# A graph network on one core: the first graph's adjacency by row block into four free banks, and matmuls of ones in PE's waits

## The reference

```python
def cheb(h, A, W, bias):              # layer 1: Chebyshev, 4 orders
    d = A.sum(-1) ** -0.5
    L = I - d[:, None] * A * d[None, :]
    P = [I, L, 2*L@L - I, 2*L@(2*L@L - I) - L]
    return sum((P[k] @ h) @ W[k] for k in range(4)) + bias

def att_layer(h, A, wv, bv, wk, bk, wq, bq):
    v, q, k = tanh(h @ wv + bv), tanh(h @ wq + bq), tanh(h @ wk + bk)
    return softmax((q @ k.T) * A - 9e15 * (1 - A)) @ v

# layer 2: h1 = tanh(h @ enc_w + enc_b); h2 = att_layer(h1); h3 = att_layer(h2);
#          a three-step MLP on [h2, h3]
# layer 3: d2 = (A.sum(-1) + 1) ** -0.5; relu((d2 * (A + I) * d2) @ h @ W)
# layer 4: t = A @ h; 1 where t > 0.5, else 0
```

## Time and profile before

| | |
|---|---|
| median of three runs | 871.86 us |
| the profiled execution | 873.75 us, its span 871.8 us |
| PE, DVE, ACT, POOL busy | 88%, 64%, 51%, 41% of the span |
| first round (graph 0 alone) | 0 to 55.8 us |
| second round | 55.8 to 104.9 us |
| a round in the middle | 49.0 us |

### The profile page before, as it was taken

How to read it: one execution, slowest core, us unless ns; L and a number is a source line. 1 busy time by engine, 2 the same in 40 slices (tenths; PEclk the granted TensorE clock), 3 DMA queues, 4 the chain that set the end, 5 groups by cost and what they waited for, 6 DMA issues and landing times.

```text
span 871.8 us, 11510 instructions
## 1 busy us (share of the span) xinstructions
PE 771.5 (88%) x3808; PEld 543.3 (62%) x3808; DVE 561.3 (64%) x1631; ACT 445.4 (51%) x929; POOL 357.0 (41%) x475
## 2 busy tenths in 40 slices
PE   3649799998999999998999999998999999998864
PEld 2426566675766766675766666675766666675533
DVE  3255667767676767767676767767676767765432
ACT  2035463737474563737474563737474563735430
POOL 3133434536162544536162544536162544532200
PEclk9869899999999999999999999999999999999995
DMA  6100100102010010201020010101020110000000
GB/s 166 45 0 1 43 14 1 61 1 61 1 61 2 21 41 0 61 1 61 1 62 1 18 44 1 61 1 62 1 61 1 18 44 1 7 1 6 1 7 6
DMA packets 29275, 22.77 MB, mean 26 GB/s; under 512 B 19488, under 2 KB 21024, under 8 KB 29216
## 3 DMA queue, kind: packets, MB, share of 16 engines
q1 hardware_dynamic: 29216, 22.03, 8.5%
HBM read 19.93 MB, written 2.10 MB: 25 GB/s over the span
## 4 chain that ended last, share of the span: by engine, by line
PE 52%; issue 16%; POOL 15%; DVE 12%; ACT 4%; POOLq 0%; DVEq 0%
PE turn_ps L1056 13%; PE pre_ps L936 8%; PE post_ps L936 4%; POOL rstd_pre L414 4%; PE pre_ps L953 4%; PE turn_ps L1039 3%; POOL k_lo L486 2%; PE pre_ps L899 2%; DVE h_nat_pre L709 2%; POOL centred_pre L417 2%; DVE score_ps L795 2%; PE qkv_ps L990 2%; DVE h_nat_pre L701 2%; PE qkv_ps L995 2%; PE post_ps L1071 2%
## 5 line engine op out<-in xcount | busy, mean ns | idle before, releaser
L589 ACT ACTIVATE negz<-negz,negmax 128x512 f32<-128x512 f32 x128 | 92.2, 720 | 63.9 <-DVE negmax L803 63.8
L414 POOL TENSOR_TENSOR rstd_post<-vareps_post,nhalf 128x4 f32<-128x4 f32 x32 | 32.8, 1024 | 209.6 <-DVE vareps_post L691 209.6
L1056 PE MATMUL turn_ps<-pt,v_n 128*128 128x512 f32 x256 | 115.2, 592 | 0.0
L795 DVE TENSOR_TENSOR score_ps<-score_ps,a_nat 128x512 f32<-128x512 f32 x128 | 89.1, 696 | 19.4 <-PE score_ps L1025 18.5
L936 PE MATMUL pre_ps<-at_hi,u_pair_pre 128*128 128x512 f32 x192 | 88.4, 461 | 7.2 <-DVE u_pair_pre L731 5.2
L548 ACT ACTIVATE y_t_pre<-pre_ps 128x512 f32<-128x512 f32 x48 | 28.7, 597 | 124.6 <-PE pre_ps L936 124.6
L803 DVE CUSTOM_DVE_ANT_0 negz<-score_ps,gate 128x512 f32<-128x512 f32 x128 | 88.6, 692 | 4.4
L414 POOL TENSOR_TENSOR rstd_pre<-vareps_pre,nhalf 128x4 f32<-128x4 f32 x32 | 33.9, 1060 | 130.7 <-DVE vareps_pre L691 130.7
L596 ACT ACTIVATE pt<-turn_ps 128x512 f32<-128x512 f32 x128 | 74.0, 592 | 17.7 <-PE turn_ps L1039 15.6
L1039 PEld LDWEIGHTS turn_ps<-ident,negz 128*128 128x128 f32 x512 | 61.1, 141 | 32.6 <-issue 16.1
L936 PE MATMUL pre_ps<-at_lo,u_pair_pre 128*128 128x512 f32 x192 | 79.3, 413 | 0.0
(11 more groups left out here) (138 smaller groups left out, 1791.5 us busy)
## 6 DMA issues: line engine op xcount, KB each, us to landing
a_nat<-in_adj SPq DMA_DIRECT2D x16, 1024.0 KB, 5.8
x_in<-in_x SPq DMA_DIRECT2D x16, 128.0 KB, 2.6
out<-x_out SPq DMA_DIRECT2D x16, 128.0 KB, 1.9
cheb_ws<-in_L_gnn_weight SPq DMA_DIRECT2D x2, 64.0 KB, 4.9
att_w<-in_L_gnn_a_wv SPq DMA_DIRECT2D x2, 64.0 KB, 2.5
att_w<-in_L_gnn_a_wk SPq DMA_DIRECT2D x2, 64.0 KB, 2.3
att_w<-in_L_gnn_a_wq SPq DMA_DIRECT2D x2, 64.0 KB, 2.2
bv_f<-in_L_gnn_a_bv SPq DMA_DIRECT2D x2, 64.0 KB, 2.7
```

Source lines behind the costliest of these rows:

```text
L414: gp.tensor_tensor(rstd[t][:], vareps[t][:], nhalf[:, 0:RB], ALU.pow)\
L589: sc.activation(probs[:, i, :], negz[:, i, :], ACT.Exp, bias=negmax[:, i:i + 1], scale=-1.0, accum_out=total[:, i:i + 1]).then_inc(probs_d ...
L795: ve.tensor_tensor(score_ps[i % 2][:], score_ps[i % 2][:], a_nat[s][:, i, :], ALU.mult)\
L1056: mm = te.matmul(turn_ps[0][:], v_n[a][:, j * P:(j + 1) * P], pt[:, j, :], start=(j == 0), stop=(j == RB - 1))
```

## The change

Five edits, of which four touch the first graph only.

1. A second table, `FIRST`, gives the order of the first round. In it ACT adds up rows first and copies the turned blocks last; DVE takes the weights' product between the splits.
2. The adjacency of graph 0 comes in four loads of one row block each, with a semaphore each. PE turns a row block as it lands, into four banks (`post_ps`, `qkv_ps`, `turn_ps`), so that a bank is complete only after the fourth row block. The transpose of h goes to `score_ps[0]`.
3. The six early weight loads are issued by ACT's queue instead of SP's. DVE's first statistics come ahead of them; the Chebyshev weights are combined behind the normalisation, the encoder's are split and the bias rows of layer 1 made behind the first fold (`cheb_fold3`), those of layer 2 behind the second.
4. `keep_busy` puts 72 matmuls of a 128x128 tile of ones with a 128x512 row of ones into PE's order of the first round, from 2 to 17 ahead of each step. They write `score_ps[1]`, which nothing reads then. POOL sets the row of ones in one more memset.
5. In every round POOL's `inverse_roots` becomes two steps: `roots` makes only the four columns that u needs, `more_roots` the rest, behind `cheb_u3`. DVE's `cheb_weights` waits for the first, `cheb_fold3` for the second.

The diff, cut to its core:

```diff
-        norm_cheb-0 add_cheb_bias-0 split_qk.1-1 mask_bias-1 inverse_roots-0 cheb_u3-0
+        norm_cheb-0 add_cheb_bias-0 split_qk.1-1 mask_bias-1 roots-0 cheb_u3-0 more_roots-0
         norm_gcn-2 split_qk.2-1 cheb_f0-0 norm_last-2 norm_enc-0
+        add_mlp_bias-0""".split(),
+}
+
+
+FIRST = {
+    "tensor": """
+        turn_a0-0 turn_a1-0 turn_a2-0 cheb_ht-0 turn_a3-0 cheb_weights-0 cheb_prop3-0 cheb_fold3-0
+        cheb_prop2-0 cheb_fold2-0 cheb_prop1-0 cheb_fold1-0 enc_ht-0 encode-0""".split(),
+    "scalar": """
+        row_sum0-0 row_sum1-0 row_sum2-0 cheb_ht-0 row_sum3-0 copy_at0-0 copy_at1-0 copy_at2-0
+        copy_at3-0 cheb_copy3-0 cheb_copy2-0 cheb_copy1-0 enc_ht-0 encode-0""".split(),
+    "vector": """
+        stats_cheb-0 norm_cheb-0 cheb_ht-0 split_at0-0 split_at1-0 cheb_weights-0 split_at2-0
+        split_at3-0 cheb_fold3-0 cheb_fold2-0 cheb_fold1-0 stats_enc-0 norm_enc-0
+        enc_ht-0""".split(),
+    "gpsimd": """
+        norm_cheb-0 add_cheb_bias-0 roots-0 cheb_u3-0 more_roots-0 cheb_f0-0 norm_enc-0
         add_mlp_bias-0""".split(),
 }
...
+        def wait_rows(eng, g, i):
+
+            if first(g):
+                eng.wait_ge(a_rows_in[i], 16)
+            else:
+                eng.wait_ge(a_loaded[g.slot], 16 * (g.round + (g.slot > 0)))
+
+        def at_bank(g, j):
+
+            return (post_ps, qkv_ps, *turn_ps)[j][:] if first(g) else pre_ps[:, j % 2, :]
+
+        def ht_bank(g, k):
+
+            return score_ps[0][:] if first(g) and k == 0 else pre_ps[:, 0, :]
...
+            order, fill = ([(entry[:-2], int(entry[-1])) for entry in table[engine]]
+                           for table in (ORDER, FIRST))
-                for name, age in order:
+                for name, age in fill if graphs[1:] == (None, None) else order:
...
-            load(Graph(0, 0), False)
+            sp.dma_start(x_in[0][:], x_d[0]).then_inc(x_loaded[0], 16)
+            for i in range(RB):
+                sp.dma_start(a_nat[0][:, i, :], adj_d[0][:, i, :]).then_inc(a_rows_in[i], 16)
             for s in range(SLOTS):
                 sp.sem_inc(x_out_free[s])
-            for to, what in early:
-                sp.dma_start(to, what).then_inc(early_in, 16)
...
+            gp.memset(ones_row[:], 1.0).then_inc(consts_done, 1)
...
-            def inverse_roots(g):
+            def roots(g):
 
                 pool.wait_ge(rowsums, 4 * g.n + 4)
+                gp.tensor_tensor(dinv[g.slot][:, 0:RB], rs[:, 0:RB], nhalf[:, 0:RB], ALU.pow)\
+                    .then_inc(root_done, 1)
+
+            def more_roots(g):
...
-                pool_pre.add(gp.tensor_tensor(d[:], rs[:], nhalf[:], ALU.pow))
+                pool_pre.add(gp.tensor_tensor(d[:, RB:], rs[:, RB:], nhalf[:, RB:], ALU.pow))
...
-                pool.wait_ge(dinv_done, g.n + 1)
+                pool.wait_ge(root_done, g.n + 1)
...
+            early = [(cheb_bs[:], cheb_b.rearrange("a b c -> (a b c)").partition_broadcast(P))]
+            early += [(half, enc_w) for half in (enc_ws[0:C], enc_ws[C:P])]
+            early += [(enc_bs[:], enc_b.rearrange("(h o) -> h o", o=1))]
+            assert len(early) == n_early
+            for half in (cheb_ws[0:C], cheb_ws[C:P]):
+                act.dma_start(half, cheb_w.rearrange("k o c d -> (o c) k d")).then_inc(cheb_in, 16)
+            for to, what in early:
+                act.dma_start(to, what).then_inc(early_in, 16)
...
+                    if i == 0 or first(g):
+                        wait_rows(act, g, i)
                     if i == 0:
-                        act.wait_ge(a_loaded[g.slot], 16 * (g.round + 1))
...
+            def split_weights(whole, high, low, made):
+
                 ve.tensor_copy(high[:], whole).then_inc(weights_split, 1)
-            dve.wait_ge(weights_split, 5)
-            for whole, high, low in splits:
+                dve.wait_ge(weights_split, made + 1)
                 ve.tensor_tensor(low[:], whole, high[:].bitcast(F32), ALU.subtract)\
                     .then_inc(weights_split, 1)
+
+            def combine_cheb_weights():
+
+                dve.wait_ge(cheb_in, 16 * n_cheb)
+                ve.scalar_tensor_tensor(cheb_ws[:, 2, :], cheb_ws[:, 3, :], 2.0, cheb_ws[:, 2, :],
+                                        ALU.mult, ALU.add).then_inc(weights_split, 1)
+                ve.tensor_tensor(cheb_ws[:, 1, :], cheb_ws[:, 1, :], cheb_ws[:, 3, :], ALU.subtract)\
+                    .then_inc(weights_split, 1)
...
             def cheb_norm(g):
                 norm_apply("pre", dve_pre, g, 0)
+                if first(g):
+                    combine_cheb_weights()
...
                 dve.wait_ge(cheb_ready, g.n + 1)
-                dve.wait_ge(dinv_done, g.n + 1)
+                dve.wait_ge(root_done, g.n + 1)
...
+                dve.wait_ge(dinv_done, g.n + 1)
...
+                if first(g):
+                    dve.wait_ge(early_in, 16 * n_early)
+                    split_weights(enc_ws[:], enc_hi, enc_lo, 5)
+                    set_bias_rows(0)
...
+                if first(g):
+                    set_bias_rows(1)
...
-            pe.wait_ge(consts_done, 7)
+            pe.wait_ge(consts_done, 8)
+
+            IDLE = {"turn_a0": 8, "turn_a1": 3, "turn_a2": 3, "cheb_ht": 2, "turn_a3": 2,
+                    "cheb_weights": 4, "cheb_prop3": 11, "cheb_fold3": 2, "cheb_prop2": 6,
+                    "cheb_fold2": 2, "cheb_prop1": 6, "cheb_fold1": 2, "enc_ht": 17, "encode": 4}
+
+            def keep_busy(g, step):
+
+                if first(g):
+                    for _ in range(IDLE[step]):
+                        te.matmul(score_ps[1][:], ones_bf[:], ones_row[:], start=True, stop=True)
+
+            def turn_first_rows(g, i):
+
+                keep_busy(g, f"turn_a{i}")
+                wait_rows(pe, g, i)
+                for j in range(RB):
+                    mm = te.transpose(at_bank(g, j)[:, i * P:(i + 1) * P],
+                                      a_nat[g.slot][:, i, j * P:(j + 1) * P], ident[:])
+                    if i == RB - 1:
+                        mm.then_inc(at_ready, 1)
 
             def turn_a(j):
                 def f(g):
-                    pe.wait_ge(a_loaded[g.slot], 16 * (g.round + 1))
-                    if j == 0 and follows(g):
-
-                        pe.wait_ge(h1_done, g.n)
+                    if first(g):
+                        turn_first_rows(g, j)
+                        return
                     if j >= 2:
                         pe.wait_ge(at_split, 4 * g.n + j - 1)
+                    wait_rows(pe, g, 0)
+                    if j == 0:
+
+                        pe.wait_ge(h1_done, g.n)
                     for i in range(RB):
-                        mm = te.transpose(pre_ps[:, j % 2, i * P:(i + 1) * P],
+                        mm = te.transpose(at_bank(g, j)[:, i * P:(i + 1) * P],
                                           a_nat[g.slot][:, i, j * P:(j + 1) * P], ident[:])
                     mm.then_inc(at_ready, 1)
                 return f
 
-            def turn_h(ready):
-
-                pe.wait_ge(h_ready["pre"], ready)
+            def turn_h(g, k):
+
+                pe.wait_ge(h_ready["pre"], 2 * g.n + k + 1)
                 for i in range(RB):
-                    mm = te.transpose(pre_ps[:, 0, i * P:(i + 1) * P],
+                    mm = te.transpose(ht_bank(g, k)[:, i * P:(i + 1) * P],
                                       h_nat["pre"][:, i, :, :].rearrange("p a c -> p (a c)"), ident[:])
                 mm.then_inc(ht_ready, 1)
 
             def cheb_ht(g):
-                pe.wait_ge(at_split, 4 * g.n + 3)
-                turn_h(2 * g.n + 1)
+                keep_busy(g, "cheb_ht")
+                if follows(g):
+                    pe.wait_ge(at_split, 4 * g.n + 3)
+                turn_h(g, 0)
 
             def cheb_weights(g):
+                keep_busy(g, "cheb_weights")
                 pe.wait_ge(ht_split, 2 * g.n + 1)
-                pe.wait_ge(at_split, 4 * g.n + 4)
                 if first(g):
-                    pe.wait_ge(weights_split, 7)
+                    pe.wait_ge(weights_split, 5)
+                else:
+                    pe.wait_ge(at_split, 4 * g.n + 4)
                 for i in range(RB):
                     w = (K - 1) * C
                     for part in (cheb_hi, cheb_lo):
@@ -955,21 +1040,35 @@
                 return mm
 
             def cheb_prop3(g):
+                keep_busy(g, "cheb_prop3")
+                if first(g):
+                    pe.wait_ge(at_split, RB)
                 pe.wait_ge(cheb_taken, 3 * g.n + 3)
                 propagate("pre", g, 3 * g.n + 1, pre_ps[:, 0, :])
 
             def cheb_prop(k):
-                return lambda g: propagate("pre", g, 3 * g.n + k, pre_ps[:, 0, :])
+                def f(g):
+                    keep_busy(g, f"cheb_prop{K - k}")
+                    propagate("pre", g, 3 * g.n + k, pre_ps[:, 0, :])
+                return f
 
             def cheb_fold(k):
```

(12 more changed lines are left out.)

83 lines of the change are left out of this document (37 added, 46 removed).

## The result

The changed kernel takes 851.72 us (median of 4 runs, 851.13 to 852.03) against 872.02 us for the kernel before in the same comparison (4 runs, 871.08 to 872.88). The ratio is 0.9767, its 95% interval 0.975 to 0.9784. The profiled execution took 851.93 us with a span of 849.8, so the two profiled executions differ by 21.8 us and the medians by 20.3; the forecast was a gain of 17.3 and 854.6 us. The direction and the parts were right; two of the three parts were undersized. So up to 1.7 us of what the profiles show as gain may belong to that one execution.

The account below looks back on a forecast made before the run. PE bounds the middle rounds; the first round is one serial chain with waits and PE at its lower clock level. Savings 6.2 + 7.7 + 3.4 + 0 = 17.3 us, from 871.86 to 854.6 us, range 850.5 to 861.

Parts of the forecast that it names:

- Part A: Program start to first propagation: earlier statistics and row-by-row turns start it at 17.6 instead of 23.86, 6.2 us saved.
- the end of h's transpose, 11.7: Before the first propagation: PE's fills, turns and transpose of h were to be over at 11.7 us.
- the early bound: Before the first propagation: if the clock rises early, at 7, 11.7 becomes 10.6 and the saving 7.3 us.
- Part B: First propagation to graph 0's tanh: same operations at the upper clock level if the fills hold it, 7.7 us saved.
- Part C: Second round: bias rows made earlier free DVE, mask0 starts 9.5 us behind the tanh instead of 12.6; 3.4 us saved.
- might go too, 2 us more: Second round, upper bound: two later slow stretches, 89.8 to 93 being one, might also vanish, 2 us beyond the 3.4.
- Part D: Every round: POOL's root in two instructions costs 0.4 us more, hidden by 11.67 us of idle time; zero effect.
- Rival 5: Every round: POOL's longer work shows, +6 us on the 17.3 saved, 860.6 us; chance 0.05.
- Rival 1: First and second rounds: clock rises early and the second round keeps it, 20.6 us saved, 851 us; chance 0.12.
- the forecast's own case: Whole kernel: 17.3 us saved, 854.6 us against the median, holding 852.5 to 857.5; chance 0.60.
- Rival 3: First round: fills hold the clock only from the first propagation on, part A gives -0.6, 861.4 us; chance 0.05.
- rival 4: First round: fills don't raise the clock and only delay PE's queue, slower than before at 875.3 us; chance 0.03.

Follow-up runs that it names:

- rows together: The changed kernel, but the first step on PE and on ACT waits for all four row blocks of the adjacency: 854.13 us, ratio 0.98.

## Why the prediction was right, and where its sizes were off

**Part A, 8.2 us instead of 6.2: the mechanism held, one term was mis-sized.** The mis-sized term is the end of h's transpose, 11.7. No run shows that value. In the changed kernel's first profile the clock rose before 6.7, the three turns and eight fills ahead of the transpose ran at 0.11 a transpose and 0.22 a fill, and the transpose was over at 10.3, even before the 10.6 that the early bound gives for a rise at 7; in its second profile it was over at 10.7. Three other kernels with the same first steps on PE (fills up to the first propagation, fills at the end, root in one piece) ran slow until nearly 9 and had it over at 11.5 to 11.6. So the size hangs on when the level rises, which differs between executions: this profile had an early one, which was luck, and with the late rise part A is 7.1 and not 8.2 (first propagation at 16.73 and 16.77). The forecast then had 5.8 us from there to the last split (17.5), and 5.3 were needed (15.59). Of the 2 us, 1.4 are the clock and 0.5 the small steps behind it. DVE set the end, as said. The order on DVE is what pays (6.5 us by the kernel with the statistics put back); fills cost part A 0.7 and only prepare part B; row blocks one by one are worth 1.9; these do not simply add up, and the four banks and ACT's new order were not tried by themselves. POOL is hidden, as said, but only by 1.0 (u ends at 14.6 and DVE at 15.6), and with the root in one piece POOL is the later by 1.8.

**Part B, 7.3 instead of 7.7: right.** The kernel with fills alone gives 7.4. The missing 0.4 is in pieces: propagations of 2.15 for 2.1, a transpose of 0.67 for 0.60, the DVE work below. The rule of the Trainium skill on the shared port pair (SBUF — State Buffer, section Who interferes with whom), which was weighed there, shows at its place: three casts of the bias rows at 27.27 take 1.69 us beside the last two of POOL's three operations (27.14 to 28.62), the same three 0.71 at 21.98 without them. By that rule it was to be up to 1 us, and it is 1.0. The last fold waited for 0.15 us of it (tmp at 31.50 instead of some 31.35). It cost next to nothing, because the slack of 1.1 us was there.

**Part C, 6.0 instead of 3.4: the step that was wrong is the one put into a bound.** mask0 starts 9.50 us behind the tanh's end, as forecast. But of the slow stretches later in that round the prediction said they "might go too, 2 us more", and left them out of the sum. In the changed kernel they are gone: 43.09 us at a clock of 1.00, against 49.09 at 0.85. From mask0 to the tanh of graph 1 that is 2.9 us less, where 0.3 was forecast. The other kernels show that most of it is the clock. The same stretch (columns as above), first in the changed kernel and then in the one with fills at the end:

```profile
80.00:84.00 4.00, 2.94 (x15) 1.85 (x15) 3.83 (x13) 2.75 (x6) 0.00 (x0) 1.00 0.00 0
80.00:84.00 4.00, 3.10 (x12) 2.71 (x13) 3.40 (x7) 1.81 (x5) 0.23 (x1) 0.57 0.00 0
```

Each of the five kernels whose only fault in this round is one such fall between 80 and 92 (rows together, root in one piece, fills at the end, statistics behind the loads, twice the fills) needs 43.9 to 44.1 us, so a fall costs 0.8 to 1.1. The kernel before has two late ones, between 88 and 96 and between 100 and 104, some 2 us; to what the rest of the 2.9 belongs is not shown. Of the others, the one with fills up to the first propagation, lower at the round's start too, needs 45.4; the three in which DVE or PE is late there as well 47.6 to 48.4. Whether the late fall comes is not decided by the table: the kernel with fills at the end has the changed kernel's code for the whole round, and it has the fall, though PE was busier just before it (2.57 us of 76 to 80, against 1.65 in the changed kernel, which keeps its level).

**Part D, nothing: right.** 588.00 against 588.40 us in twelve rounds, and the root in one piece changes them by 0.2. Rival 5 is out.

**The rivals.** Rival 1, "the clock rises early and the second round keeps it", is what happened: it gave 20.6 us and 851, and 20.3 and 851.7 came. It had 0.12, and the forecast's own case, which had 0.60, was to hold 852.5 to 857.5: the measured time lies 0.8 us outside it. What spoke against rival 1, two gaps that remain, was true of the gaps and false of their result. Rival 3 (fills hold the clock only from the first propagation on) is refuted by the turns at 6.70, rival 4 by everything from there. The whole lies inside the range, 2.9 us under the forecast. That it is no more is partly luck: the three parts gave 21.5 us in the profiles where 17.3 was forecast, and the medians differ by less than the profiles do. One reading of the page was wrong without a consequence: of the first five slices of the clock three are low, not four.

What stays open: which activity exactly lets the clock fall at 84 in one kernel and not in another that has the same instructions in that round. No run here was made to settle it.

## What to carry to other kernels

Where one chain of small steps was alone, most of its matmuls ran at half rate, and matmuls without a use in its waits doubled it: 72 of them gave 9.8 us at the start, 54 gave 4.2 in the stretch at the end. The 9.8 count only together with the new order; on the kernel before the same fills gave 6.7. Count them so that they end before the real work comes, since the surplus is paid at 0.216 us each (twice the fills: all the gain of the fills lost). And a wait that is made longer has a second price, the clock that falls in it: a POOL chain that ended 1.8 us behind DVE made the next propagation 1.2 us longer too.

## What the runs showed of the chip beyond that

- The granted clock of the first microseconds reads 1.00 while the matmuls run at the lower level. In the stretch 0 to 15.6 of the changed kernel the column says 1.00, and its first eight fills take 0.42 us each (3.37/8) where later ones take 0.216. The spacing of equal matmuls is the measure there.
- The moment of the first rise differs between executions. In the changed kernel's first profile turn 0 is fast at 6.70; in others of the same first steps (fills at the end, root in one piece) turn 0, at 6.88, still took 0.21 a transpose, and the first transposes 0.11 apart come at 8.88 and 8.99. With fills at the end the first propagation then starts at 16.73 instead of 15.63.
- The level can be lost between two propagations: in the kernel with fills only up to the first propagation the second propagation, 5.7 us behind the start of the fast one, is slow again, with one fold (1.12 us of PE) and 2.4 us without PE between them.
- DVE's tensor_tensor that splits u takes 0.82 us beside POOL's c_diff (26.52) and 0.43 without it (20.84). The Trainium skill (SBUF — State Buffer, section Who interferes with whom) says that a DVE instruction with two SBUF inputs contends with a GpSimd one that reads SBUF; the trace agrees.
